# Retention attention and a mixture-of-experts FFN: the attention part unrolled, its order, state sums, y and W_o scaling and weight preparation changed

## The reference

```python
q, k, v = (layernorm(x) @ W.T for W in (W_q, W_k, W_v))
attn = einsum('bihd,bjhd->bhij', q, k) * gamma[h] ** (i - j) (0 where i < j) / 4
y = einsum('bhij,bjhd->bihd', attn, v)
yn = (y - mean) / sqrt(var + eps)      # per batch and head, over all tokens and the head's channels
x = x + (yn * gn_weight + gn_bias) @ W_o.T
xf = layernorm(x)
shared = (silu(xf @ sw1 + sb1) * (xf @ sw3 + sb3)) @ sw2 + sb2
out = mean over 2 of 8 experts, chosen by (11 * token + k * 7919) % 8, of gelu(xf @ w1[e] + b1[e]) @ w2[e] + b2[e]
x = x + (shared + out) / 2
```

## Time and profile before

| | |
|---|---|
| median of 3 runs | 503.66 us (502.91 to 506.73) |
| the profiled execution's own time | 502.85 us |
| its span in the trace | 501.1 us |
| busy share PE, weight load, DVE, ACT, POOL | 91%, 85%, 58%, 45%, 16% |
| matmuls, weight loads | 6558, 6558 |

### The profile page before, as it was taken

How to read it: one execution, slowest core, us unless ns; L and a number is a source line. 1 busy time by engine, 2 the same in 40 slices (tenths; PEclk the granted TensorE clock), 3 DMA queues, 4 the chain that set the end, 5 groups by cost and what they waited for, 6 DMA issues and landing times.

```text
span 501.1 us, 14986 instructions
## 1 busy us (share of the span) xinstructions
PE 458.3 (91%) x6558; PEld 423.9 (85%) x6558; DVE 292.5 (58%) x606; ACT 223.5 (45%) x412; POOL 79.6 (16%) x61
## 2 busy tenths in 40 slices
PE   6979999769988799799779499999999999999997
PEld 4969989769977799798658399988998899988997
DVE  6554666545774466748899854365734756436321
ACT  2544538305473145633557253436343472524531
POOL 2040001200030000401547011030200301011000
PEclk8979989979998799989999799999999999999999
DMA  8940000050000600006500401040012200130011
GB/s 285 410 157 24 24 25 24 3 192 25 24 24 29 245 9 3 3 14 234 220 1 1 160 9 44 33 178 0 0 42 95 114 0 0 42 126 1 0 43 43
DMA packets 9321, 36.38 MB, mean 73 GB/s; under 512 B 1584, under 2 KB 2352, under 8 KB 6832
## 3 DMA queue, kind: packets, MB, share of 16 engines
q1 hardware_dynamic: 8832, 34.72, 18.5%
q10 hardware_dynamic: 432, 0.79, 0.5%
HBM read 27.11 MB, written 8.39 MB: 71 GB/s over the span
## 4 chain that ended last, share of the span: by engine, by line
PE 73%; DVE 13%; issue 8%; ACT 3%; POOL 2%; DMA 1%; SPq 0%; DVEq 0%; POOLq 0%; ACTq 0%
PE bank L271 55%; PE bank L340 5%; PE bank L357 3%; PE bank L383 3%; PE bank L373 3%; DVE pm L798 3%; PE bank L282 2%; PE bank L327 2%; DMA xin<-xa 1%; POOL slot_bias L1121 1%; PE bank L452 1%; DVE ln_st L764 1%; DVE xlo L784 1%; DVE kT L791 1%; DVE ylo L849 1%
## 5 line engine op out<-in xcount | busy, mean ns | idle before, releaser
L271 PE MATMUL bank<-x2hi,sw_hi 128*128 128x512 f32 x128 | 51.6, 403 | 9.8 <-DVE gf L935 7.6
L577 ACT ACTIVATE vexp<-bank 64x256 f32<-64x256 f32 x64 | 24.2, 378 | 73.7 <-PE bank L271 73.1
L681 ACT ACTIVATE xres<-bank,r1b 128x256 f32<-128x256 f32 x64 | 26.7, 469 | 58.5 <-PE bank L271 58.5
L271 PE MATMUL bank<-x2hi,sw_lo 128*128 128x512 f32 x128 | 51.3, 401 | 0.0
L271 PE MATMUL bank<-x2lo,sw_hi 128*128 128x512 f32 x128 | 50.8, 396 | 0.0
L340 PE MATMUL bank<-qT,keo 32*128 32x64 f32 x1024 | 38.0, 298 | 11.7 <-issue 11.7
L340 PEld LDWEIGHTS bank<-qT,keo 32*128 32x128 f32 x1024 | 35.5, 210 | 14.7 <-issue 14.1
L798 DVE TENSOR_TENSOR pm<-bank,msk 128x512 f32<-128x512 f32 x64 | 39.7, 682 | 12.4 <-PE bank L340 12.4
L666 ACT ACTIVATE sil<-bank,s1b 128x512 f32<-128x512 f32 x32 | 22.0, 688 | 49.0 <-PE bank L271 49.0
L935 DVE SCALAR_TENSOR_TENSOR gf<-bank,s3b,sil 128x512 f32<-128x512 f32 x32 | 23.9, 747 | 30.3 <-PE bank L271 30.3
L271 PEld LDWEIGHTS bank<-x2hi,sw_hi 128*128 128x128 f32 x128 | 24.3, 190 | 17.1 <-DVE gf L935 8.5
(11 more groups left out here) (120 smaller groups left out, 1285.5 us busy)
## 6 DMA issues: line engine op xcount, KB each, us to landing
xin<-xa SPq DMA_DIRECT2D x16, 256.0 KB, 4.4
xres<-xs SPq DMA_DIRECT2D x4, 1024.0 KB, 4.9
w_raw<-w SPq DMA_DIRECT2D x2, 2048.0 KB, 13.2
x_scratch<-xres SPq DMA_DIRECT2D x4, 1024.0 KB, 6.7
xr<-x_scratch SPq DMA_DIRECT2D x4, 1024.0 KB, 4.9
xl<-x_scratch SPq DMA_DIRECT2D x4, 1024.0 KB, 6.9
out<-xr SPq DMA_DIRECT2D x8, 512.0 KB, 2.6
dec<-decay SPq DMA_DIRECT2D x1, 1536.0 KB, 11.2
```

The costliest lines, as they stand in the source:

```text
L271: mm = nc.tensor.matmul(o, w[c][l], x[c][r], start=first and c == 0 and j == 0, stop=last and c == n - 1 and j == 2)
L577: cp = nc.scalar.activation(dst[64 * h2:64 * h2 + 64, :, f, :, h2, :], src[64 * f:64 * f + 64, :, :, h2, :], ACT.Copy)
L681: ge = nc.scalar.activation(hf[q % 2][:, m, :], e_bank[q % 4][:, m * 2 * P:(m + 1) * 2 * P], ACT.Gelu, bias=r1b[:, e, m:m + 1])
```

## The change

- The attention's loops are gone: on every engine all 16 steps are written out with constant waits.
- PE's order within a step is now v, k, q of h+1, transposed k, transposed x of h+2, (bias or output parts), from_state(h), from_scores(h), state_sums(h+1), scores(h+1).
- `state_sums` makes a chunk's product 2 or 1 slots wide, in the bank of q; DVE adds the two pairs one after the other, and a state is carried to the next part times `fade` (gamma to the 256th), so that `dec` holds 256 positions (512 KB).
- y has a bank of its own. ACT and DVE split it directly from the bank, unnormalised, part by part; its statistics are read from the bank as well. `yT`, `yn`, `y0` and the POOL copy are gone.
- The normalisation's scale goes onto W_o (`high_wo`, `low_wo`, once a batch), its offset through a product of W_o with the spread bias (`output_bias`), copied by ACT to `o_bias`, which POOL adds to the residual (`bias_xres`, four instructions of 128x512 a batch).
- Outputs: two of four parts in the third step of the next batch, two in its fourth. For batch 3, parts come after shared(0, 3).
- The FFN weights are loaded in 11 pieces of 512 KB behind the x loads and split one a step in steps 0 to 10, the high part on ACT (with a scaling pass for sw2 and w2), the low part on POOL. The bias sums of POOL move to step 1, two DVE instructions for them to steps 2 and 3.
- SP's order on its queue: x0, masks, x1, dec, x2, x3, gn, x4, sw1, x5, sw3, the biases b2 and sb2, x6, W_o, small biases, x7, w1 piece 0, x8, piece 1, x9, piece 2, residual 0, x10, w1 piece 3, x11, sw2, x12, w2 piece 0, x13, piece 1, store batch 0, residual 1, x14, piece 2, x15, piece 3, store batch 1, residual 2; x(h) waits until the transposes of part h-4 are done.

```diff
-            dec = sb_1("dec", [P, 2, GROUPS, T])
+            dec = sb_1("dec", [P, 2, GROUPS, SUPER])
...
+            state = [sb_1(f"state{i}", [P, GROUPS, CPS + 1, 32]) for i in range(2)]
...
+                b, s = h // NSUP, h % NSUP
+                if b and s == 1:
+                    pe.wait_ge(gn_ve, b)
+                elif b and s == 2:
+                    pe.wait_ge(ob_copied, b)
+                elif b and s == 3:
+                    pe.wait_ge(x1_ready, (b - 1) * 4 + 2)
+                elif b > 1:
+                    pe.wait_ge(x1_ready, (b - 1) * 4)
...
-                if not (isinstance(h, int) and h == 0):
-                    pe.wait_ge(y_copied, h)
+                pe.wait_ge(qT_ready, h + 1)
                 for c in range(CPS):
-                    n = CPS - c
...
-                            mm = nc.tensor.matmul(sy_bank[32 * p:32 * p + 32, o:o + n * 32].rearrange("p (n e) -> p n e", n=n),
-                                                  kexp[:, c, r, :], vexp[s % 2][:, c, r, :].unsqueeze(1).broadcast_to([P, n, 32]),
+                            mm = nc.tensor.matmul(b_bank[32 * p:32 * p + 32, o:o + n * 32].rearrange("p (n e) -> p n e", n=n),
+                                                  kexp[:, c, r, :], vexp[h % 2][:, c, r, :].unsqueeze(1).broadcast_to([P, n, 32]),
...
-                pe.sem_inc(pe_passed, 1)
-                first = 0 if s else 1
+                if h:
+                    pe.wait_ge(y_stats, h)
...
+            def output_bias(b, bank):
+                pe.wait_ge(bb_ready, b + 1)
+                for c in range(CB):
+                    mm = nc.tensor.matmul(bank[:, 0:D], y_bb[:, c, :], wo_raw[:, c, :], start=(c == 0), stop=(c == CB - 1))
+                mm.then_inc(ob_done, 1)
...
-            with pe.Fori(0, NBATCH - 1) as b:
-                step(b, 2)
-                step(b, 3)
-                step(b + 1, 0, norm=True)
-                step(b + 1, 1, out=True)
-            step(NBATCH - 1, 2)
-            step(NBATCH - 1, 3)
...
+            for h in range(PARTS):
+                step(h)
...
+                dve.wait_ge(s_first, h + 1)
+                nc.vector.tensor_tensor(now[:, :, 3:5, :], sums[:, :, 2:4, :],
+                                        now[:, :, 2, :].unsqueeze(2).broadcast_to([P, GROUPS, 2, 32]), ALU.add).then_inc(s_ready, 1)
+                if s < NSUP - 1:
+                    dve.wait_ge(s_ready, h + 1)
+                    for g in range(GROUPS):
+                        ts = nc.vector.tensor_scalar(then[:, g, 0, :], now[:, g, CPS, :], fade[:, g:g + 1], None, ALU.mult)
+                    ts.then_inc(s_carried, 1)
```

More of the change, by code:

```diff
@@ L17 @@
 NSUP = T // SUPER
+PARTS = NBATCH * NSUP
 TILES = SUPER // P
@@ new lines, in _ @@
+            load_x(7)
+            load_ffn(2)
+            load_x(8)
+            load_ffn(3)
+            load_x(9)
+            load_ffn(4)
+            next_xres(0)
+            for h in range(10, 14):
+                load_x(h)
+                load_ffn(h - 5)
+            store_x1(0)
+            next_xres(1)
+            load_x(14)
+            load_ffn(9)
+            load_x(15)
+            load_ffn(10)
+            store_x1(1)
+            next_xres(2)
+            sp.wait_ge(t_done, PARTS)
@@ L431, in step @@
-                from_state(b, s)
-                if out:
-                    for j in range(2, 4):
-                        pe.wait_ge(pm_ready, g * PAIRS + (j + 1))
-                        output(b - 1, j, p_bank[j])
-                from_scores(b, s)
-                if more[2]:
-                    transpose_x(*ahead(b, s, 2))
-                if norm:
-                    pe.wait_ge(gn_ve, b)
-                if out:
-                    pe.wait_ge(x1_ready, b * 4)
+                if b and s == 1:
+                    pe.wait_ge(pm_ready, h * PAIRS + 2)
+                    output_bias(b - 1, p_bank[1])
@@ L607, in normalise_y @@
-            def normalise_y(b):
-                act.wait_ge(gn_ready, b + 1)
-                act.wait_ge(y0_moved, b + 1)
-                for g in range(GROUPS):
-                    nc.scalar.activation(yn[:, g, :].rearrange("p (s k u) -> p s k u", s=NE, k=CPB),
-                                         yT[:, g, :].rearrange("p (k s u) -> p s k u", s=NE, k=CPB),
-                                         ACT.Identity, bias=y_b[:, g:g + 1], scale=y_a[:, g:g + 1]).then_inc(yn_ready, 1)
-            def high_y(b, g):
-                act.wait_ge(yn_ready, b * GROUPS + (g + 1))
-                nc.scalar.activation(yhi[:, g, :], yn[:, g, :], ACT.Copy).then_inc(yhi_ready, 1)
@@ L805, in add_state @@
                 if s == 0:
[L806 removed]
+                    nc.vector.tensor_copy(now[:, :, 1:3, :], sums[:, :, 0:2, :]).then_inc(s_first, 1)
                 else:
[L808 to L810 removed]
@@ new lines, in bias_xres, with low_ffn @@
+            def bias_xres(b):
+                pool.wait_ge(xres_landed, (b + 1) * 16)
+                pool.wait_ge(ob_copied, b + 1)
+                for j in range(4):
+                    part = xres[:, 2 * j:2 * j + 2, :]
+                    nc.gpsimd.tensor_tensor(part, part, o_bias[:].unsqueeze(1).broadcast_to([P, 2, D]), ALU.add).then_inc(xres_biased, 1)
+            def low_ffn(i):
+                w, at = ffn_piece(i)
+                passed(ffn_hi, i + 1)
+                nc.gpsimd.tensor_tensor(w.lo[:, at], w.raw[:, at], w.hi[:, at].bitcast(F32), ALU.subtract).then_inc(ffn_lo, 1)
```

644 lines of the change are left out of this document (246 added, 398 removed).

## The result

The changed kernel took 512.9 us (median of 4 runs, 511.2 to 515.3) against 503.3 of the kernel before: 1.018 times the time, 95% interval 1.012 to 1.025. It is slower, by 1 to 2.5%; forecast were 465 us. The first fence is from the page of the changed kernel, its profiled execution.

A forecast was written before the change was run, and what follows sets the result against it. PE was taken to bound an ordinary step. Stages 20.0 + 150 + 17.9 + 38.3 + 214.3 = 440.5 us, plus fetch 15, clock 4, other 3 gave 462.5 span, plus 1.75 outside and 0.8 for the median: 465 us, range 446 to 490.

The forecast's parts named there:

- 24 output products take 2.85 us, so 48 take 5.7: Attention outputs: products keep their duration from the old trace, 5.7 us of the 6.9 us extras a batch.
- I get 1.0 us a step, 15 us: Dense small products in each attention step: PE waits for instruction packets, 15 us in all, bounds 0 and 25.
- 3.0 to 3.8 us from request to use: Instruction fetch: time from asking for the next packet until PE can use it, read from the old trace.
- all this: 3 us: Other engines, DMA waits and data transfers that delay instruction packets: 3 us together (0 to 15).
- I charge 4 us (0 to 15): PE's clock falling behind its remaining, shorter stalls: 4 us (0 to 15).
- State sums: Ordinary attention step: widths 2, 1, 2, 1 take 0.70 us instead of 1.16, so 0.46 less.
- shape changes: Ordinary attention step: tile shape changes go from six to four, saving 0.3 us (0.2 to 0.4).
- loops: Attention written out: the issue stalls of 4.4 us where PE's loop turns back vanish.
- passage: Last attention step and passage to the experts: 38.3 us together, bound by PE.
- PE wants the masked scores 5.5 us later, so it is covered: Attention step: DVE held by POOL's 2.4 us operation delays masks without holding PE; worst case a step of 10.9 us.
- Rival 1: Instruction fetch in the attention is hidden: 448 us, chance 0.22.
- Rival 3: Slower: stalls every step keep TensorE at 1.2 GHz, losing 44 us to reach 509, 88 us of attention work at half speed; chance 0.04.

The follow-up runs named there:

- e1: Changed kernel with ACT and DVE storing the split y slot by slot, so output products load contiguous weights; 489.1 us.
- e6: e1 with PE's old order: x transposes between from_scores and the new scores, scores ahead of the state sums; 502.8 us.
- e2: Changed kernel with from_state and from_scores taken out of the dense block and spread between PE's projections; 503.4 us.
- e12: Changed kernel with 32 more small products of zeros (128 recorded instructions) in the warm-up; 515.1 us.
- e3: Changed kernel with SP issuing x, weight pieces, stores and residuals after the scores instead of after the transposes; 496.5 us.
- e15: e10 with DVE's fade of the carried state moved behind kT and SP's transfers issued after the scores; 468.2 us.
- e11: Kernel before the change with only TensorE's loop over three batches written out; 495.6 us.
- e5: Changed kernel with the edits of e1 and e3 together; 480.9 us.
- e4: Changed kernel with the edits of e1, e2 and e3 together; 489.0 us.
- e9: e5 with TensorE's small products regrouped in two blocks and DVE adding states ahead of the low part of y; 489.8 us.
- e10: e6 with DVE's residuals moved ahead of the low part of x; 485.5 us.
- e16: e5 with DVE's fade of the carried state moved behind kT; 474.5 us.
- e13: e10 with POOL writing zeros instead of subtracting for the low parts of the FFN weights; 475.7 us.
- e8: Changed kernel with 128 increments of an unread semaphore ahead of TensorE's program; 531.3 us.

## Why the prediction was wrong

The forecast's span was 462.5 us, the measured one 509.3. The 46.8 us between them, by its own steps:

- **"24 output products take 2.85 us, so 48 take 5.7".** The step that failed first, and by the most. The duration came from a row of the kernel before, whose weights lie one after another; the changed line reads them eight elements apart, and that stood in the diff. Measured: 5.79 us, eight times, 23.5 us more. e1 undid it alone and got 23.8.
- **"I get 1.0 us a step, 15 us", bounds 0 and 25.** The mechanism was right (e6 and e2: another order, no stalls; e12: the edge moves), the term was mis-sized: it measured 24.9 us, at the bound, 9.9 more. The 3.0 to 3.8 us from request to use, taken from a quiet window, hold where no data flows (3.4 at 118 us). Amid data it was up to 6.0, which stood under "all this: 3 us". e3 got 11 of the 24.9 back by timing transfers alone.
- **Clock: "I charge 4 us (0 to 15)", with 3 for the rest.** The third term that was mis-sized. What remains, 46.8 - 23.5 - 9.9 = 13.4 us, is beyond these 7, so 20.4 in all, and nearly all of it is the clock. The windows of single steps show it, here a step without a slow stretch and one with:

```profile
57.00:70.56 13.56, 10.30 (x301) 9.80 (x301) 11.04 (x25) 6.50 (x13) 3.04 (x2) 1.00 0.41 138
...
87.00:103.60 16.60, 14.08 (x306) 13.29 (x305) 12.68 (x23) 6.77 (x14) 7.47 (x6) 0.81 0.16 50
```

  A clock of 0.92 over 225 us [the window above] means 36 us at 1.2 GHz, worth at most 18, for the 4 charged. In the chain seven groups of 36 projections behind a stall take 6.0 to 6.9 us in place of 4.51, 13.1 us too much together, and the scores behind the stalls some 5 more (estimate from the same rows). That leaves 2 to 4 us for small waits, as the 3 charged had it. The argument was that shorter stalls make the clock fall less. The longest fell from 4.4 to 3.3 us, but there are fifteen issue waits in place of six, and the clock stands at 0.92, for 0.93 in the earlier trace rows. In e3, with issue stalls of at most 1.8 us, it was 0.96, in e2, with 0.4 us of them, 0.99.
- **State sums, shape changes, loops, passage.** Right: 0.70 us; two changes of shape fewer give 0.28 us a step for the 0.30 charged (the sums take 0.70 for 0.83 where they follow the scores in e15, the transposes of x 0.44 for 0.59 in the earlier trace rows); a step without stalls 10.1 us; the stalls of 4.4 us gone (e11: 6.8 us by itself); TensorE without long waits in the passage; and the last stage unchanged.
- **"PE wants the masked scores 5.5 us later, so it is covered".** Right in the changed kernel, with 1.6 us of waits for pm, where the stalls themselves gave DVE time. With shorter stalls in the same order waits for kT come (2.4 us in e3, 4.9 in e5), and in other orders (e2, e4, e6, e9, e10) 21 to 34 us of waits, most of them for DVE. That is also why 23.8 + 16.4 saved singly made 32 together (e5); e16, with the fade moved, brings it to 38.
- **The rivals.** Rival 1, a hidden fetch, is refuted by the 24.9 us of issue. The Trainium skill, "Runtime: NRT & Kernel Launch", section Instruction fetch mechanics, calls the crossing mostly hidden; the traces of e2 and e6 agree (0.4 and 1.4 us), that of the changed kernel doesn't. Its densest 256 instructions, from_scores with the state sums, are used up in 1.7 us. Rival 3 had the right side by the wrong road, and 512.9 next to its 509 is luck: it asked for 88 us at 1.2 GHz, and there were 36. No rival had a product that changed its own duration.

With the first two terms put right (23.5 and 9.9) the forecast would have read 498 us, 1% under the kernel before; the 13.4 us of clock and small waits then put it on the other side.

## What to carry to other kernels

Before a duration is taken over from the old trace, compare each operand's access pattern in the diff: a "same" product with its weights eight elements apart cost twice as much, and the write is the better place for the stride. Small tiled products can use up instructions faster than they are fetched, so lay long operations between their groups and issue transfers where TensorE is in long ones, and then look again at what the stalls had been hiding. Where an in-order engine can be held by a neighbour, put its exposed operation where the neighbour is idle, and not ahead of what others wait for.

## What the runs showed that was not expected

- A weight load of 128x128 with a stride of eight elements takes 337 ns for 188 to 191 contiguous, and the product's pitch goes from 0.12 to 0.24 us. Writing with neighbours 128 elements apart (e1) costs ACT 1080 ns for 597 and DVE 1047 for 690 (128x512).
- A DVE operation on 128x32 elements of SBUF stood until a POOL subtraction ended: 2.56 us for two, against 0.24 each. A POOL memset of 0.95 us held it as well (e13, 1.1 us). The Trainium skill, "SBUF — State Buffer", section SBUF: two separate sides, says that DVE and GpSimd share a pair of ports, which some operations of DVE need and which one instruction holds to its end; these rows agree.
- An increment of a semaphore on TensorE cost 0.15 us (127 from 0.81 to 20.08 us, e8), more than a pair of weight load and product in a projection (4.51/36 = 0.125).
- The clock fell behind waits of TensorE whoever caused them: in e6, with 1.4 us of issue but 34 of waits for DVE and ACT, up to 3.5 us long, it was 0.91 from 20 to 245 us, lower than in the changed kernel. Not every wait did it: in e2, with 26 us of waits and none over 2.6 us, it was 0.99.
